# A macaron transformer block stack on one core: the row sums of the first layer's feed-forward normalisation on ScalarE in place of VectorE, with the orders of all queues written anew

## The reference

```python
def _layernorm(x, axis=-1, eps=1e-05):
    m = jnp.mean(x, axis=axis, keepdims=True)
    v = jnp.var(x, axis=axis, keepdims=True)
    return (x - m) / jnp.sqrt(v + eps)
...
x = x + 0.5 * _L0_ffn_ref(_layernorm(x, axis=-1), ...)   # 256 -> 704 -> 256, silu(gate) * up, integer weights with scales
x = x + _L0_attn_ref(_layernorm(x, axis=-1), ...)        # 16 heads of 16, rotary embedding, causal softmax
x = x + 0.5 * _L0_ffn_ref(_layernorm(x, axis=-1), ...)
x = x + 0.5 * _L1_ffn_ref(_layernorm(x, axis=-1), ...)   # sigmoid(gate) * up, ternary weights
x = x + _L1_attn_ref(_layernorm(x, axis=-1), ...)        # 16 query heads, 4 key heads, linear bias by distance
x = x + 0.5 * _L1_ffn_ref(_layernorm(x, axis=-1), ...)
```

## Time and profile before

| | |
|---|---|
| median of three runs | 553.93 us (552.02 to 555.36) |
| the profiled execution's own time | 552.14 us |
| its span, first to last instruction | 550.4 us |
| granted TensorE clock, mean | 1.000 of full speed |
| instructions | 12977 |
| engine busy | PE 530.6 us, DVE 456.1, ACT 401.3, POOL 340.8, PEld 302.9 |

### The profile page before, as it was taken

How to read it: one execution, slowest core, us unless ns; L and a number is a source line. 1 busy time by engine, 2 the same in 40 slices (tenths; PEclk the granted TensorE clock), 3 DMA queues, 4 the chain that set the end, 5 groups by cost and what they waited for, 6 DMA issues and landing times.

```text
span 550.4 us, 12977 instructions
## 1 busy us (share of the span) xinstructions
PE 530.6 (96%) x5060; PEld 302.9 (55%) x5060; DVE 456.1 (83%) x816; ACT 401.3 (73%) x603; POOL 340.8 (62%) x427
## 2 busy tenths in 40 slices
PE   8999798999999999999899999999999999999997
PEld 6676444445554654566446564465455654654664
DVE  5999999998989797699987969879997779783363
ACT  5978594878777698775886848788769676969443
POOL 2549896975987797673664364552855626545634
PEclk9999999999999999999999999999999999999999
DMA  8900110302130100410110120010211011101211
GB/s 324 355 1 2 58 58 2 116 23 62 41 103 18 43 1 2 157 42 20 63 43 2 42 83 22 22 43 6 75 36 43 1 42 64 52 2 62 80 58 38
DMA packets 22573, 31.76 MB, mean 58 GB/s; under 512 B 9408, under 2 KB 10816, under 8 KB 22360
## 3 DMA queue, kind: packets, MB, share of 16 engines
q1 hardware_dynamic: 22512, 30.94, 16.4%
HBM read 13.75 MB, written 2.36 MB: 29 GB/s over the span
## 4 chain that ended last, share of the span: by engine, by line
PE 71%; DVE 17%; ACT 4%; issue 3%; POOL 2%; SPq 1%; DMA 0%; DVEq 0%; POOLq 0%; ACTq 0%
PE PS L597 22%; PE PS L621 12%; PE PS L708 10%; PE PS L688 5%; PE PS L673 5%; DVE MX L1064 5%; PE PS L639 4%; PE PS L723 4%; PE PS L580 3%; PE PS L544 2%; PE PS L559 2%; ACT PB L850 2%; PE PS L655 2%; DVE MX L1060 1%; DVE ST L875 1%
## 5 line engine op out<-in xcount | busy, mean ns | idle before, releaser
L850 ACT ACTIVATE PB<-PS 128x1024 f32<-128x1024 f32 x160 | 158.7, 1025 | 52.9 <-PE PS L688 48.4
L1064 DVE TENSOR_REDUCE MX<-PS 128x2 f16<-128x1024 f32 (+2 forms) x192 | 158.3, 865 | 13.8 <-PE PS L544 13.1
L597 PE MATMUL PS<-XT,WGU 128*128 128x512 f16 x660 | 156.9, 380 | 4.6 <-DVE QF L1042 3.0
L1140 POOL TENSOR_TENSOR HH<-TH,HH 128x512 f16<-128x512 f32 x71 | 82.5, 1173 | 69.0 <-ACT HH L818 69.0
L1168 POOL TENSOR_SCALAR_AFFINE_SELECT PB<-PB 128x512 f32<-128x512 f32 (+1 forms) x140 | 73.8, 552 | 48.1 <-ACT PB L850 47.9
L597 PEld LDWEIGHTS PS<-XT,WGU 128*128 128x128 f16 x660 | 59.6, 98 | 75.9 <-issue 7.8
L621 PE MATMUL PS<-WD,HH 128*128 128x256 f16 x660 | 78.2, 273 | 0.4 <-POOL HH L1140 0.2
L708 PE MATMUL PS<-PB,V 128*32 128x512 f32 (+3 forms) x1024 | 75.3, 435 | 0.8 <-ACT PB L850 0.3
L621 PEld LDWEIGHTS PS<-WD,HH 128*128 128x128 f16 x660 | 62.6, 98 | 13.3 <-issue 3.3
L818 ACT ACTIVATE HH<-TH 128x512 f16<-128x512 f32 (+1 forms) x86 | 52.9, 628 | 20.2 <-PE PS L621 6.9
L673 PE MATMUL PS<-SK,SQ 63*128 63x256 f16 (+3 forms) x512 | 59.5, 299 | 5.3 <-DVE MX L1064 2.6
(11 more groups left out here) (119 smaller groups left out, 777.7 us busy)
## 6 DMA issues: line engine op xcount, KB each, us to landing
SQ<-QPB SPq DMA_DIRECT2D x24, 256.0 KB, 2.5
OC<-OT SPq DMA_DIRECT2D x16, 256.0 KB, 2.4
RB<-scratch SPq DMA_DIRECT2D x64, 64.0 KB, 2.3
SK<-QPB SPq DMA_DIRECT2D x12, 256.0 KB, 2.4
SQ<-MT SPq DMA_DIRECT2D x128, 1.0 KB
out<-X SPq DMA_DIRECT2D x8, 256.0 KB, 2.1
PB<-gu SPq DMA_DIRECT2D x2, 704.0 KB, 6.1
LATE<-gu SPq DMA_DIRECT2D x2, 704.0 KB, 14.5
```

The lines of the kernel that those rows point to most:

```text
L597: m = e.matmul(o[:, :], WGU[l][:, k, col:col + P], rows_of(f)[j][:, k, :], start=j == 0 and k == 0, stop=j == 1 and k == 1)
L850: e.activation(PB[Q % 2][:, j, :, :], two_banks("s", i), ACT.Exp, scale=0.25).then_inc(a_exp, 1)
L1064: e.tensor_reduce(mx[:, :, pr, t], o[:, :, col:col + (t + 1) * P], AX.X, ALU.max, negate=True).then_inc(a_max, 1)
L1140: e.tensor_tensor(hh[1][:, s * T:(s + 1) * T], value_of(j)[0], hh[0][:, s * T:(s + 1) * T], ALU.subtract).then_inc(f_lo, 1)
```

## The change

It takes the two grouped sums out of step N. ScalarE gets a new step m, once for each of the eight first-layer units: four activations with the function Copy, one for each tile of 128x256, that write a half-precision copy nobody reads (JUNK) and have the running sum of the row put into one column of FM (`accum_out`). Each of the four waits for the one before it. POOL's offset now waits for the four sums instead of for DVE's. All strings of ORDER, with the banks, are new; apart from ACT's eight m they hold the same letters, each as often as before. On ACT the dummy silu T stands first.

```diff
-LNF = [10 if l == 0 else 8 for _, l, _ in FFNS]
+LNF = [8] * NF
...
 ORDER = {
     "sp":
-        "kkrrkrkrDSrRDSRrrkDSkrRrDSRrrrkDSRkDSRrlrkkrDrSRrDSRrkklrDrSRrDSrRrkkrDrSRrDSRrDrkSkrDRSrRrrODSRDSOR"
+        "kkrrrkkrDSrRDSRrrkDkSrRrDSRrrrDkSRkDSRrrlkkrDrSrRlDSRkrrkDrrSRDSrRrkkrDrDSRrSRrkrDkrSDRSrRrOOrDSRDSO"
...
     "pe":
-        "zzzzzzzttzgGgggGGgGtzztgzGzagGgddddggGztzzgzGtGuugGaqqvgddgdvdqgGgqgtGGGguuGtqqqzmmmgmmgqmmdmmGsdsms"
+        "zzzzzzzttzGggggGgGgGtGtzzgGzagddddggGgtzzzGGuuzatgqqgzgddqgddggvGgvqGGGtuutGqqqmmzmgmmdmgmmdqsmGsms"
...
     "dve":
-        "NXgwttNhhkhhNhtwwwtwhwhwdwwdwhnhNtwhkwuuhthpqwpqwdwdpnhqpqhhkhuuhhqpttqpmmmsmhmsxmmmpmqdmpxmhqmmmsmx"
+        "NXgttwNhhhkhNhthtwwwhwwdwhdwNnkhwwwhwhuutwtphpqqwdpwdqnhhpqhkhhuuhtqpptqmmmmmmxpsmmdsqmhmxmhpmmqmsmd"
...
     "act":
-        "wXxxTwttthtXhhthxxhtwwhtthwXthwtxwthYyyxthkhhkkvwQttQXtktvkhtYQyytQhhhxxkkkhhtwTQteQeeeeteewQQhoeete"
+        "TmwXxxmttthtXtthhxhxhwhtwmwtwXtthtmYwyyxhxhthwhhttkQwkQkttkvXtvQhhYtyyQxxhhkwkThkhQttkQeeeeehetQeQho"
...
-        FM = sb("FM", [P, 68])
+        FM = sb("FM", [P, NT])
+        JUNK = sb("JUNK", [P, D], F16)
...
+                elif c == "m":
+                    f = [j for j in range(NF) if FFNS[j][1] == 0][i]
+                    b, l, was = unit_x(f)
+                    w.wait_ge(f_mean, f)
+                    for t in range(NT):
+                        wait_x(w, b, l, was, t // 2)
+                        w.wait_ge(f_fm, NT * i + t)
+                        e.activation(JUNK[:, :], X[:, NT * b + t, :], ACT.Copy, accum_out=FM[:, t:t + 1]).then_inc(f_fm, 1)
...
-                if fine:
-                    e.tensor_reduce(FM[:, 0:64], xv.rearrange("p t (a c) -> p (t a) c", c=16), AX.X, ALU.add).then_inc(ln, 1)
-                    w.wait_ge(ln, base + 2 * NT + 1)
-                    e.tensor_reduce(FM[:, 64:68], FM[:, 0:64].rearrange("p (t a) -> p t a", t=NT), AX.X, ALU.add).then_inc(ln, 1)
...
-                    w.wait_ge(f_ln, LNF0[i] + 2 * NT)
+                    w.wait_ge(f_ln, LNF0[i + 1])
...
                     if l == 0:
-                        w.wait_ge(f_ln, LNF0[i + 1])
-                        e.tensor_scalar(OFF[0][:, :], FM[:, 64:68], -1.0 / D, None, ALU.mult).then_inc(f_mean, 1)
+                        w.wait_ge(f_fm, NT * before(i, 0) + NT)
+                        e.tensor_scalar(OFF[0][:, :], FM[:, :], -1.0 / D, None, ALU.mult).then_inc(f_mean, 1)
```

More of the change, by code:

```diff
@@ L110 @@
     "sp":
-        "kkrrkrkrDSrRDSRrrkDSkrRrDSRrrrkDSRkDSRrlrkkrDrSRrDSRrkklrDrSRrDSrRrkkrDrSRrDSRrDrkSkrDRSrRrrODSRDSOR"
-        "OOOOOO",
+        "kkrrrkkrDSrRDSRrrkDkSrRrDSRrrrDkSRkDSRrrlkkrDrSrRlDSRkrrkDrrSRDSrRrkkrDrDSRrSRrkrDkrSDRSrRrOOrDSRDSO"
+        "ROOOOO",
     "pe":
-        "zzzzzzzttzgGgggGGgGtzztgzGzagGgddddggGztzzgzGtGuugGaqqvgddgdvdqgGgqgtGGGguuGtqqqzmmmgmmgqmmdmmGsdsms"
-        "msdsmgmmsdsmmpmssgmsGsGsmspsmsgmmGmpsmssmsgmmsGmmpsmsvmsvsmsmuummpqssqosmoomssoddsmqqmspttmsdgggsGdG"
@@ L116 @@
[L116 to L120, removed]
@@ L121 @@
-        "ggGgGGooooddddttgggGgGGgGGgdddd",
-    "dve":
-        "NXgwttNhhkhhNhtwwwtwhwhwdwwdwhnhNtwhkwuuhthpqwpqwdwdpnhqpqhhkhuuhhqpttqpmmmsmhmsxmmmpmqdmpxmhqmmmsmx"
[L124 to L128, removed]
@@ L129 @@
-    "act":
-        "wXxxTwttthtXhhthxxhtwwhtthwXthwtxwthYyyxthkhhkkvwQttQXtktvkhtYQyytQhhhxxkkkhhtwTQteQeeeeteewQQhoeete"
[L131 to L135, removed]
+        "zzzzzzzttzGggggGgGgGtGtzzgGzagddddggGgGtzzzGGuuzatgqqgzgddqgddggvGgvqGGGtuutGqqqmmzmgmmdmgmmdqsmGsms"
@@ new lines @@
+        "msdsmdmsgmmmspmssGsmgsGssmpmsmgsmGmpssmsmsgmmsGmmpsmsvsmvmsmsuummpqqsmsoossmoossqqsmddmpttdsmgggsGdG"
+        "sgmmmpsmmsGmsgsgmsmGGpsmvdsmdmsmvssduudqsspmmooqttoosmsggsmqmGgGsgGgmspmsgsmGGstqtpsssddgssddGggpmmm"
+        "gvmGGggGmvummGuoooosmqsmqssmqsmmdmmdddsmsmssmmspmmsmttsspmsgGggGgGmsgGgGmpmstdmstdssddsmsggmmpsmgvGg"
+        "uuGsqmsqgGqGmsgGoommpddmmsdmsdsmsososmmpmsttmsggsgGssmGmpsmgGsmsgGsmGgmmspssmvdmmsddsmsdmsspsmttoogm"
+        "smoogugGuGsqmsmqqsmggGgGGmsmpmssdmmsdmsdmsdmspsmsmsmpsmttvsggmmGgGgGgGssmgGmtssddddmsppsmtoouuogsmqm"
@@ new lines @@
+        "soqssqggGsssGspmsmgmmvGmpmmgmgmsGmssGsmtstmmpmmsddddgoosoosmsgsmGmsgGmmspsssGgggssspssGGttpGgddggdgd"
+        "GgGgGooGooddddttGgggGgGgGGgdddd",
+    "dve":
+        "NXgttwNhhhkhNhthtwwwhwwdwhdwNnkhwwwhwhuutwtphpqqwdpwdqnhhpqhkhhuuhtqpptqmmmmmmxpsmmdsqmhmxmhpmmqmsmd"
+        "xmmkhmsnhmmxmmmshmcmxmmmsmhmcmmmuxummpqxpmqmoopqNmpmqdttmschshxskdhmmsmmmhmsxmmshhnmcmdmxmuudNpqmmop"
+        "qttomhxmpmhNkqhmhmmxhhptqctsdhdnshksmmcmshhmshmxsmuhuoommmllmmxmmdmldmmxNmmmmmNtxtmhhkhmhhmhmtcxmdtd"
+        "mnmmsmhcshsuuhklmslhlxshmsohmmdmmxmdmNommmxttNhmmkhmmhhxcmmhmhmmxcmmdmdmnmttxommosshhuushmmllkmlsshx"
+        "shhmmmmmmxdmdmNmcmmNttmxhmhckhmhhmhtmddxnmmotuumhmlxoNlklhhcmmmmmxhmmmmhmchxmmmtmmdtxhdoomNmmhmhmxkh"
+        "chhtthcddhhkhhohoNdXttdhhhkhhhdd",
@@ new lines @@
+    "act":
+        "TmwXxxmttthtXtthhxhxhwhtwmwtwXtthtmYwyyxhxhthwhhttkQwkQkttkvXtvQhhYtyyQxxhhkwkThkhQttkQeeeeehetQeQho"
+        "eeeteehehoeewtoeeeeehtYoeevheveecyyoceeeeQemeeQXxoxeQtQtethehtoeeheteethchoheveYeeeyycveeoXxxQeettem"
+        "hQtehtetXeehohetxhhQxeoeeteeQhttohtYchthtvhycyvehQeQeeeQeeeeeoXexxeemtoththethetXhthhoexeexeeettoeYv"
+        "htyyecQthecQtQhhethhoeeeeeeXoxxeettetheemeotheehtehthehoeveXeceeeecoxxeYetttyyhheQheQeQttthhheoeeeee"
+        "eoeeeXoexxevtXththththehtehecxeeocYoexyyetQehQeeQtteeeeoheXthvotteeeeehhhxcoxecteeeethetXheheoetetee"
+        "eeexthxhhoottcthhcthththhXxxtththhtthhth",
@@ L136 @@
     "pool":
-        "wwwrrhrhhhhddewhwhhhshasraqdqdseasaqqhhshahhswaqqsffasfadfqdqffhfhffwehfffcfhffChcCsfsaafrfqqssaaqqd"
-        "fffhdchfffhhhefdCfcdfrCsasfafrfqsqhahfffhhhsafqqffhceChcChfhhdffdfrffbrhhfffhhhcfffehChchCbhhdfdffrf"
-        "ffhfhcffrhhhCcfCehffhfbhhfhfdfdffrcrhhfhhhfcCfeCffffhfrfhbhhhcfcCCrffhffffffhchhhCchChhhhrhhhhh",
+        "wwwrrhhhhhrdwderwhhhhhsasasdqqdaesaqqhshhhhasqasawfqffdsaqdfffqhfhffwefffhhfchffCcCssaaqfffrqssaaqqd"
+        "fffhfhcffhdhhefCdfcfdCrsafqsaffsrhaqfhffhhhsqfafqfechhCcChhhfdffdffrfrfbfhfhhhhfffceCchhChhhdfdffrff"
@@ L141 @@
+        "fhfhffhhhrccCCeffhfhfhhhfffddffrbrhchhhhcbfffeCCfffrffhfhchhhCcCbffrfhfhfffffhhhcCchChhhhrhhhhh",
     "banks":
[L142 to L145, removed]
@@ L146 @@
-        "5436116351361064526045602745275103651365203705346134724064202407136570146342176043416056314064725042"
-        "0570242054205264026046345160435063257607506341601253750264276240735631041654025603502365036525027025"
-        "40264502720452062120537203610413463042672046032503464315275046357372145632576341240",
+        "7324612231056423625371423073436465012765101356624307152563460143501326015405614640630206162062462526"
+        "2642602426042572450270537502360426024502725013501536042762046420650624063142027325063106460720462064"
@@ new lines @@
+        "2035623065131460351630165423160165436204632065076203740520356034602670246724061301460143627632630573"
+        "5362403640263056306406240625351370513462140530642374201357136310136526046036415073246302653167035120"
+        "3620540634046264031604630513754206530623504702575317064172042504625410426157314610315745215024520640"
+        "2570245041561064026412476013705240743206432056247143752403567135037402407305237503751045315427054206"
+        "40256402720572146563056246053604235073452064206721657417024761405237235064136051402",
@@ L251, in macaron_kernel @@
         p_act, p_pool, p_dve, p_pe, p_set, p_tab, p_sc, p_gu = (sem(f"p_{n}") for n in ("act", "pool", "dve", "pe", "set", "tab", "sc", "gu"))
-        f_ln, f_ve, f_mean, f_rt, f_off, f_xn, f_xd = (sem(f"f_{n}") for n in ("ln", "ve", "mean", "rt", "off", "xn", "xd"))
+        f_ln, f_fm, f_ve, f_mean, f_rt, f_off, f_xn, f_xd = (sem(f"f_{n}") for n in ("ln", "fm", "ve", "mean", "rt", "off", "xn", "xd"))
         f_turn, f_xhi, f_xlo = sem("f_turn"), sem("f_xhi"), sem("f_xlo")
@@ L869, in vector_program, with ln_stats @@
             w, at = Once(e), Counter()
-            def ln_stats(z, ln, base, wait_in, xv, fine):
+            def ln_stats(z, ln, base, wait_in, xv):
                 for t in range(NT):
@@ L889, in vector_program @@
                     w.wait_ge(f_off, i)
-                    ln_stats(0, f_ln, LNF0[i], lambda pair: wait_x(w, b, l, was, pair), X[:, NT * b:NT * b + NT, :], l == 0)
+                    ln_stats(0, f_ln, LNF0[i], lambda pair: wait_x(w, b, l, was, pair), X[:, NT * b:NT * b + NT, :])
                 elif c == "X":
@@ L905, in vector_program @@
                     w.wait_ge(a_off, i)
-                    ln_stats(1, a_ln, LNA0[i], lambda pair: wait_x(w, b, l, "ffn", pair), X[:, NT * b:NT * b + NT, :], False)
+                    ln_stats(1, a_ln, LNA0[i], lambda pair: wait_x(w, b, l, "ffn", pair), X[:, NT * b:NT * b + NT, :])
                 elif c == "w":
```

## The result

The changed kernel takes 556.52 us (median of 11 runs) where the kernel before takes 553.41 us beside it (11 runs). The ratio is 1.0058 (95% interval 1.0041 to 1.0075), so it is slower by 3.1 us, where I had forecast 3.5 us faster. (One of the 11 took 2487.74 us and is not in the ratio.) The profiled execution has a span of 555.6 us against 550.4. Those spans are 5.2 us apart and the medians 3.1. One part of that is chance: the profiled execution of the change lies 0.8 us above its median. Another is TensorE's granted clock. The other ten runs of the changed kernel are all at 0.999 or 1.000, with a median of 556.5 us. At the same clock the change is thus 4.1 us slower.

The account below looks back on a forecast made before the run. DVE was taken to bound the kernel up to 108 us and PE behind; 1.4 + 1.4 + 0.7 = 3.5 us gained on DVE, other terms at 0, gave 553.93 - 3.5 = 550.4 us, range 546.9 to 557.0.

Parts of the forecast that it names:

- What bounds the kernel: DVE bounds ahead of 108 us, PE behind; sums removed ahead of 108 us gain 3.5 us.
- What is moved: Reordered strings of all engines: milestones hardly shift, cost 0, at most 1.8 us once for SP's moved DMAs.
- What is removed and added: Eight units: DVE loses 1.4 us of sums each (11.2 us); ACT gains blocks of 2.2 us each (17.6 us).
- T first pays for the block of unit 1: ACT's opening: table load of 1.28 us and dummy of 0.2 move into idle time, making room for that block.
- What now waits: POOL's offset waits for ACT's sums, and ACT's exponentials stand behind copies; both costed at 0.
- The signs that I named: Profile signs: DVE full from 12 us, PE takes the chain near 104 us, no new PE waits for ACT behind.
- The sign of a wrong root: DVE waiting for ACT over 2 us between 12 and 35 us, or ACT reloading its table for a summing copy.
- (a): Opening: ACT's blocks of units 1 and 2 delay silus, leaving 1.4 us gain or less; 552.5 us, chance 0.26.
- (c): Behind 108 us: late ACT blocks hold up exponentials and PE, net +4.1 us; 558.0 us, chance 0.17.
- (b): Behind 108 us: two of four late sums on DVE's chain also count, 2.8 us more; 547.6 us, chance 0.14.
- (d): First three units: sums arrive after POOL's power, X later by what DVE saves; 553.9 us, chance 0.03.
- The rule that I weighed: Plain arithmetic belongs on VectorE, factor up to about three in bf16; a block near 4.2 us, 34 us in all.

Follow-up runs that it names:

- Experiment 3: Kernel before, in its old orders, with the grouped sums left out and nothing in their place, mean from the statistics: 551.98 us, ratio 0.9972.
- experiment 4: Changed kernel in its new orders, without the steps m and without sums, mean from the statistics: 556.93 us, ratio 1.0065.
- experiment 15: Changed kernel with SP's four DMAs for the denominators' way back put ahead of four row copies: 561.89 us, ratio 1.0155.
- experiment 1: The change's code in the orders of the kernel before, the eight m put into the old ACT string: 562.07 us, ratio 1.0151.

## Why the prediction was wrong

**What bounds the kernel: the step that failed first.** "DVE is full from 12 to 108 us, so a sum there is worth its full time" gave 3.5 us. Experiment 3 measured 0.4 us by the first exponential and at the end 1.5 by the medians, 1.0 by the spans. Two things stood for the bound that were none: a busy share that contained waiting beside POOL, and a chain that ran along DVE because it follows whichever engine ended last. Rows of my own view showed POOL at 38.63 of 43 us; I never asked what DVE's next wait would be. Unit 3's sum was on the chain itself, and its removal bought 0.4 us at most, since POOL was just behind.

**What is moved: the step that set the sign.** I counted letters between milestones, found them the same and wrote 0, with at most 1.8 us once. Experiments 3 and 4 measured 5.1 us, enough alone to turn a gain of 3.5 into a loss. The counts themselves were right (72 and 112 steps on DVE in both orders). But a count of steps ahead of a milestone does not see how long before its use a step is issued; experiment 15 shows 4.7 us for one letter that no count would notice. The clock was in no term either: a stall of PE was priced at its length, and in experiment 15 the added stall cost twice that.

**What is removed and added: right in size.** L880 and L882 are gone. The block took 2.04 us for 2.2, ACT is busy for 414.4 us for 417, copy and read together fall in 410 to 650 ns. DVE is at 449.2 us for 445; without any sums it is at 445.5 in the old orders and at 448.4 in the new ones (experiments 3 and 4), with 800 instructions in both, so longer instructions under the new orders are most of the rest. The table serves the copies without another load. "T first pays for the block of unit 1" held in the old orders: 1.2 us at the first exponential, and 0 without a block.

**What now waits: 0 was right under the new orders** (experiment 4) and wrong by 9.9 us under the old ones (experiment 1 against 3): a cost of the placing, not of the work.

**The signs that I named.** PE takes over the chain at 102.2 us, earlier than my 104, and the kernel is slower all the same: the handover is no milestone, a fixed step such as the first output copy is. The sign of a wrong root, DVE waiting for ACT by more than 2 us between 12 and 35 us, did not come: DVE has 2.65 us of holes there for 0.48, but 1.1 of them wait for ACT and the others for PE, and experiment 3 has as many (20.31 busy of 23) with no block on ACT. The signs would have passed a forecast that was wrong.

**The rivals.** (a) named a loss of the early gain through ACT; the gain was lost, to POOL. (c) had the sign and a time of 558.0; its mechanism shows in experiment 1, for two of four blocks, and not in the change, where PE has no stall over 0.35 us at the late blocks (147, 205, 277 and 348 us) that the kernel without blocks has not too. (b) and (d) did not occur. The measured 556.5 us lies inside the range that I gave, near its upper end of 557.0; that end was drawn for (c), so it is luck.

**The rule that I weighed**, of the Trainium skill's page "ScalarE: Activation LUTs", gave an estimate of 4.2 us for a block; they took 2.04, so by the f32 rows it was rightly set aside. The rule of the Trainium skill's page "SBUF — State Buffer" on the shared ports, which spoke to the step that failed, I left out.

## What to carry to other kernels

Before pricing a removal on a "full" engine, look at that engine's instructions of one shape: if the same shape takes 573 or 1664 ns, its busy time holds waiting; then look at the engine beside it in the same way, for the bound may be the two together. Price a new order by the time between each step's inputs and its use, not by counts of steps, and give it a wide term of its own: in this kernel one letter was worth 4.7 us and the whole rewriting 5.1, both more than the 3.5 that I had hoped to gain. Where a change makes or removes a stall of PE of some microseconds, read the granted clock of all executions beside it: in experiment 15 it cost as much again as the added stall, and runs of the kernel before at a lower clock made this comparison 1 us milder than it is at the same clock. When code and order change together, the reverse half (new orders with old code, old orders with new code) says which of them the time belongs to.

## What was new about the hardware

An activation with a running sum comes as two instructions, 417 ns and 186 ns for 128x256, with a pitch of 0.54 us. DVE and POOL stretch each other's instructions: two 128x2 operations took DVE 2.45 us, a 128x4 power took POOL 1.94 us for 1.04, a 128x512 addition 2.92 us for 1.28. Behind a stall of PE of 3.5 us TensorE ran at 1.2 in place of 2.4 GHz until 378 us (experiment 15), which cost about as much again as the added stall.
